# Expert loop of a decoder layer: ids and tables of a block loaded by SyncE, table loads behind the down products, first splits in the last row

## The chip, the cores and the metric

The kernel runs on one core of a Trainium2 chip. The metric is the time of one execution on the device in microseconds, the median of three runs. The engines are TensorE (PE; PEld is its weight load), VectorE (DVE), ScalarE (ACT), GpSimd (POOL) and SyncE (SP), each with its own queue of instructions worked off in order, and 16 DMA engines that carry out the transfers which SP, ACT and POOL issue. Engines wait for one another by semaphores; a DMA adds 16 to its semaphore when it has landed.

## The reference

The input is `x` of 4 rows of 512 tokens with 512 features. The layer adds multi-query attention (16 heads), a selective state-space scan, and a mixture of experts. Only the last part is touched by the change:

```python
logits = x @ gate_weight.T                       # 2048 tokens, 32 experts
topv, topi = jax.lax.top_k(softmax(logits), 8)   # some of the 8 are dropped (weight under 0.05)
...
def expert_step(acc, xs):                        # for each of the 32 experts
    w_gu, w_d, c_e = xs
    g, u = jnp.split(x @ w_gu.T, 2, axis=-1)     # 512 -> 2 x 192
    h = jax.nn.silu(g) * u
    return acc + h @ w_d.T * c_e[:, None], None  # 192 -> 512, times the token's weight
```

## The kernel before

The first part of the program (1373 us) works through the four batch rows: attention, scan and routing of a row, with the next row's beginnings between. At a row's end the tokens are routed: GpSimd scatters an entry for each of a token's choices (`send`, line 1583: 33 floats, namely the token's 32 weights and its number as a float) into `lists`, a table in DRAM with a stretch for each expert. The scatters of the last row come in eight groups `sent0` to `sent7` of four (`send_last`); group k holds each token's k-th choice, counted from the lowest expert, so the list of expert e is complete after groups 0 to e.

The expert loop then works through the lists in blocks of 128 tokens. An expert has at least two blocks; there are 68 here, in 17 quads of four. Which expert and which rows of `lists` a block has is known only at run time: VectorE computes the tables `tab` and `blocks` (in SBUF, line 1508), and every engine reads its loop counts and indices from them by a table load (`value_load`, a load of one number into a register by the engine's queue).

What each engine does for block n:

- SyncE, `load_quad`: loads the 128 entries of each of a quad's four blocks into `meta` (line 429), which has room for all blocks. It may run ahead of the loop, one quad in flight at a time.
- VectorE, `next_ids`: copies the token numbers of block n+4 from `meta` to `get_ids` as whole numbers.
- GpSimd, line 1617 (`get`): gathers the tokens' rows from `xf_dram` into slot n % 4 of `x_blk`, four blocks ahead; line 1623 (`add`): adds the finished rows of `y_ring` to `out` in DRAM by a DMA that accumulates. An add waits until the add two blocks before has landed; the first add of an expert waits until all earlier ones have landed, since a token can be in several experts' lists.
- TensorE, `quad`: at the head of a quad five table loads (line 783), then for each block: `gate_up` of block n+1 (12 matmuls in three parts of split precision, lines 760 to 762), `xt`, the transposes of block n+2 (line 451), `down` of block n (five matmuls, lines 775 to 779), `ht`, the transposes of the hidden values of block n+1.
- ScalarE: `silu`, `xt` (high part of the transposed block), `weigh` (line 1091 copies the ids for the add, line 1093 writes the weighted result to `y_ring`), `ht`. For every expert it also splits the weights, `w_hi` from `w_raw` (line 1073), and issues the weight loads (`load_part`, line 973: 384 and 896 KB), each behind a wait for the load before.
- VectorE: low parts `xt_lo`, `ht_lo`, `w_lo` (`split`, line 1514), and `hidden`, the product of the two halves.

The weights of expert e are loaded four experts ahead, split three (ScalarE) and two (VectorE) ahead. Those of the first experts are loaded in the last row, but split after it, when the routing is done.

Of the kernel before, what the change touches and what calls it, by code (L numbers as in the profile page):

```python
# [26 lines left out]
P = 128  # L27
# [20 lines left out]
T_MORE, T_BEFORE, T_LAST = 0, NE, 2 * NE  # L48
# [28 lines left out]
EXP_BLK = NTOK // P + QUAD - 1  # L77
MAX_BLK = (NTOK * TOPK // P + MIN_BLK * NE + QUAD - 1) // QUAD * QUAD
# [26 lines left out]
def constants():  # L105
# [12 lines left out]
    c[:, C_ALL + NE::LIST_COLS] = NTOK + (p[:, None] * PADS + np.arange(PADS)[None, :]) % P  # L118
# [3 lines left out]
def decoder_layer(nc, a):  # L122
    ctx = ExitStack()
    with ctx:
# [9 lines left out]
        bank = [ctx.enter_context(nc.psum_tensor(f"bank{i}", [P, 512], F32)) for i in range(8)]  # L134
# [31 lines left out]
        xn_hi, xn_lo = sb("xn_hi", [P, KT, T], F32R), sb("xn_lo", [P, KT, T], F32R)  # L166

# [11 lines left out]


        k_t = sb("k_t", [P, T])
        k_hi, k_lo = sb("k_hi", [P, T], F32R), sb("k_lo", [P, T], F32R)
        v_aug = sb("v_aug", [P, TT, DH + 1])
        q_s = sb("q_s", [P, TT, 4, DH])
        q_t = sb("q_t", [P, 2, T])
        q_hi, q_lo = sb("q_hi", [P, 2, T], F32R), sb("q_lo", [P, 2, T], F32R)
        probs = sb("probs", [P, KT, T])
        o_s = sb("o_s", [P, TT, DH])
        k_n = o_s
        o_t = sb("o_t", [P, H, T])  # L190
        wout = sb("wout", [P, 4, D])
        delta = sb("delta", [P, ET, T])
        du = sb("du", [P, ET, T])
        y = sb("y", [P, ET, T])
        decay = sb("decay", [P, ET * (T + DC - 1)])
        x_pad = decay[:, :].rearrange("p (e t) -> p e t", e=ET)
        dA = decay[:, 0:ET * T]
        dA3 = dA.rearrange("p (e t) -> p e t", e=ET)
        dbu = sb("dbu", [P, ET, T])
        state = sb("state", [P, ET, T])  # L200
        b_bc = sb("b_bc", [P, 2, T])
        c_bc = sb("c_bc", [P, 2, T])
        x_dbl = sb("x_dbl", [XD, T])
        junk = sb("junk", [P, 4, DH], mybir.dt.bfloat16)
# [32 lines left out]
        def sb(name, shape, dt=F32):  # L237
# [8 lines left out]
        meta = sb("meta", [P, MAX_BLK + EXP_BLK + QUAD + 1, LIST_COLS])  # L246
        get_ids, add_ids = sb("get_ids", [P, QUAD], I32), sb("add_ids", [P, QUAD], I32)
        xt_hi, xt_lo = sb("xt_hi", [P, KT, P], F32R), sb("xt_lo", [P, KT, P], F32R)
# [21 lines left out]
            w_in meta_in blk_in0 blk_in1 blk_in2 blk_in3  # L270
# [3 lines left out]
            carry_ok ids_ok added0 added1  # L274
# [25 lines left out]
        def span(eng, e):  # L300

            return (eng.value_load(tab[0:1, bass.ds(e, 1)], min_val=MIN_BLK - 1, max_val=EXP_BLK - 1),
                    eng.value_load(tab[0:1, bass.ds(e + T_BEFORE, 1)], min_val=0, max_val=MAX_BLK))

# [16 lines left out]
        def _(sp):  # L321
# [101 lines left out]
            def load_quad(q):  # L423

                rows = [sp.value_load(blocks[0:1, bass.ds(q * QUAD + (B_ROW + i), 1)], min_val=0, max_val=LIST_ROWS - P) for i in range(QUAD)]
                if not (isinstance(q, int) and q == 0):
                    wait_apart(sp, S["meta_in"], q * (QUAD * 16))
                for i in range(QUAD):
                    sp.dma_start(meta[:, bass.ds(q * QUAD + i, 1), :].rearrange("p o c -> p (o c)"), lists[bass.ds(rows[i], P), :]).then_inc(S["meta_in"], 16)
# [5 lines left out]
            early = TOPK * MIN_BLK // QUAD  # L435
            for q in range(early):
                for k in range(QUAD // MIN_BLK * q, QUAD // MIN_BLK * (q + 1)):
                    sp.wait_ge(S[f"sent{k}"], TT * 16)
                load_quad(q)
            with sp.Fori(early, last_quad + 2) as q:  # L440
                load_quad(q)

            wait_apart(sp, S["meta_in"], last_quad * (QUAD * 16) + 2 * QUAD * 16)
            sp.wait_ge(S["w_in"], NE * 2 * 16)
# [4 lines left out]
        def _(pe):  # L449
# [289 lines left out]
            xt_bank, gu_bank, ht_bank, y_bank = bank_q[0], bank_s[0], bank_s[1], bank_o[0]  # L739
            pe.wait_ge(S["carry_ok"], NB)  # L740
            pe.matmul(bank_q[1][:, 0:NE], ones, carry[:], start=True, stop=True).then_inc(S["cnt_ps"], 1)
# [6 lines left out]
            def xt(q, r):  # L748

                wait_apart(pe, S[f"blk_in{r}"], q * 16 + 16)  # L750
                for k in range(KT):
                    mm = transpose(xt_bank[:, k * P:(k + 1) * P], x_blk[:, r, k * P:(k + 1) * P])
                mm.then_inc(S["xt_ps"], 1)

            def gate_up(blk, e):
                hi, lo = gate_up_w(w_hi, e), gate_up_w(w_lo, e)
                pe.wait_ge(S["wlo_ok"], e * 2 + 2)
                pe.wait_ge(S["xtlo_ok"], blk + 1)
                for k in range(KT):
                    pe.matmul(gu_bank[:, 0:2 * INTER], xt_hi[:, k, :], hi[:, k, :], start=(k == 0), stop=False)  # L760
                    pe.matmul(gu_bank[:, 0:2 * INTER], xt_hi[:, k, :], lo[:, k, :], start=False, stop=False)  # L761
                    mm = pe.matmul(gu_bank[:, 0:2 * INTER], xt_lo[:, k, :], hi[:, k, :], start=False, stop=(k == KT - 1))  # L762
                mm.then_inc(S["gu_ps"], 1)
# [17 lines left out]
            def quad(q, last):  # L781

                es = [pe.value_load(blocks[0:1, bass.ds(q * QUAD + (B_EXPERT + i), 1)], min_val=0, max_val=NE - 1) for i in range(QUAD + 1)]
                for r in range(QUAD):
                    blk = q * QUAD + r
                    ends = last and r == QUAD - 1
                    if not ends:
                        gate_up(blk + 1, es[r + 1])
                        xt(q + (r + 2) // QUAD, (r + 2) % QUAD)
                    down(blk, es[r])  # L790
                    if not ends:
                        ht(blk + 1)

# [3 lines left out]
            first = pe.value_load(blocks[0:1, B_EXPERT:B_EXPERT + 1], min_val=0, max_val=NE - 1)  # L797
            xt(0, 0)
            gate_up(0, first)
            xt(0, 1)  # L800
            ht(0)
# [5 lines left out]
        def _(act):  # L807
# [161 lines left out]
            def load_part(e, part):  # L969

                if not (isinstance(e, int) and e + part == 0):
                    act.wait_ge(S["w_in"], (e * 2 + part) * 16)
                act.dma_start(part_w(w_raw, e, part, N_RAW),
                              a["w_exp"][bass.ds(e, 1), :, W_PARTS[part][0]:W_PARTS[part][1]].rearrange("o p n -> (o p) n")).then_inc(S["w_in"], 16)
# [36 lines left out]
            def row(b, at, last):  # L1011
# [57 lines left out]
            xt_bank, gu_bank, ht_bank, y_bank = bank_q[0], bank_s[0], bank_s[1], bank_o[0]  # L1069

            def split(e, part):
                act.wait_ge(S["w_in"], (e * 2 + part + 1) * 16)
                act.activation(part_w(w_hi, e, part, N_SPLIT), part_w(w_raw, e, part, N_RAW), ACT.Copy).then_inc(S["whi_ok"], 1)

            def xt(blk):
                act.wait_ge(S["xt_ps"], blk + 1)
# [617 lines left out]
```

## Time and profile before

| | |
|---|---|
| median of three runs | 1858.85 us (1858.75 to 1859.49) |
| profiled execution: its time | 1863.07 us |
| its span, first to last instruction | 1861.3 us |
| TensorE busy over the span | 80% |
| VectorE busy | 70% |
| ScalarE busy | 51% |
| GpSimd busy | 26% |
| granted TensorE clock, mean | 0.887 |

The times in the rows are microseconds from the first instruction of the one profiled execution. In the timeline a row has the start, the length, engine, line of the kernel, operation, what is written from what, and in brackets how long the engine was idle before and what it waited for; "issue" is a wait for nothing that the profile shows. An engine's name with a q is its queue. A row of the windows view gives the stretch, its length, the busy time of PE, PEld, DVE, ACT and POOL with the number of instructions, the granted TensorE clock as a share of 2.4 GHz, the DMA engines' busy share and GB/s.

### The profile page before, as it was taken

The page shows a single profiled execution, that of the slowest core. Times are in us where ns is not written, and L with a number is a line of the kernel's source. Part 1 is how long each engine was busy: PE and PEld are TensorE (multiplying, and loading weights), DVE is VectorE, ACT ScalarE, POOL GpSimd, SP SyncE. Part 2 cuts the span into 40 slices and gives each one's busy share as a digit, 9 for nine tenths or more (in the row PEclk, how much of TensorE's full clock was granted, in tenths as well). Part 3 has the DMA queues.
Part 4 walks back from the last instruction along what each step waited for, and adds up shares of the span by engine and source line. Part 5 has one row for each costly group of instructions (what it writes and reads, how often), then busy time and mean ns, then how long its engine had stood idle before and what let it go on. Part 6 is the DMA issues. An engine that isn't in the chain of part 4 may idle for free.

```text
span 1861.3 us, 27828 instructions
## 1 busy us (share of the span) xinstructions
PE 1480.5 (80%) x6758; PEld 1056.7 (57%) x6759; DVE 1306.4 (70%) x1908; ACT 954.9 (51%) x2447; POOL 489.8 (26%) x309
## 2 busy tenths in 40 slices
PE   4888889769888986888899597889535777787776
PEld 1677655357665534676654475664224666666664
DVE  6599987559998846899874687986452455555553
ACT  4677743337775244677624465762122444554543
POOL 0000000008700000880000078000036444444454
PEclk8899999869999985999998598999756988988898
DMA  6783231223333113134221413215102777676764
GB/s 250 263 234 85 85 95 41 80 94 73 92 100 85 46 47 131 40 88 114 87 62 34 149 37 82 79 45 157 62 24 58 180 177 191 166 174 166 170 147 58
DMA packets 96495, 202.28 MB, mean 109 GB/s; under 512 B 24984, under 2 KB 26473, under 8 KB 95264
## 3 DMA queue, kind: packets, MB, share of 16 engines
q1 hardware_dynamic: 54960, 86.66, 16.2%
q0 software_dynamic: 28000, 63.84, 14.4%
q10 hardware_dynamic: 13456, 50.87, 9.3%
q8 instruction: 33, 0.54, 0.1%
q14 instruction: 46, 0.38, 0.1%
HBM read 171.06 MB, written 46.21 MB: 117 GB/s over the span
## 4 chain that ended last, share of the span: by engine, by line
DVE 32%; PE 30%; issue 21%; ACT 8%; POOL 2%; DMA 2%; DVEq 2%; ACTq 1%; SPq 0%; another core or an unknown queue 0%; POOLq 0%
DVE state L1267 10%; PE bank L634 8%; DVE y L1277 6%; DVE dbu L1272 5%; PE bank L451 4%; PE bank L760 3%; POOL lists L1583 2%; PE bank L761 2%; PE bank L762 2%; PE bank L594 2%; DVE dbu L1261 2%; DMA w_raw<-in_w_exp 2%; ACT decay L911 1%; PE bank L662 1%; PE bank L518 1%
## 5 line engine op out<-in xcount | busy, mean ns | idle before, releaser
L1583 POOL DMA_INDIRECT lists<-entry,slot x128 | 262.8, 2054 | 395.1 <-DVE slot L1455 207.0
L1267 DVE TENSOR_TENSOR_SCAN state<-decay,dbu 128x2048 f32<-128x2048 f32 x64 | 282.5, 4415 | 7.3 <-ACT decay L911 2.8
L594 PE MATMUL bank<-v_aug,probs 128*128 128x129 f32 x2048 | 250.2, 281 | 7.2 <-ACT probs L905 7.2
L594 PEld LDWEIGHTS bank<-v_aug,probs 128*128 128x128 f32 x2048 | 243.7, 196 | 18.2 <-ACT probs L905 15.2
L634 PE MATMUL bank<-wout,o_t 128*128 128x512 f32 x512 | 234.3, 612 | 0.0
L905 ACT ACTIVATE probs<-bank 128x512 f32<-128x512 f32 x256 | 146.5, 609 | 167.9 <-PE bank L576 129.6
L1579 POOL DMA_DIRECT2D wq<-wq_dram x30 | 21.7, 727 | 735.8 <-PE bank L528 668.7
L911 ACT ACTIVATE decay<-delta,neg_a 128x511 f32<-128x511 f32 x256 | 163.9, 728 | 27.4 <-DVE state L1267 27.4
L760 PE MATMUL bank<-w_hi,xt_hi 128*128 x272 | 113.3, 417 | 81.2 <-issue 58.5
L1623 POOL DMA_INDIRECT out<-y_ring,add_ids x68 | 120.3, 1769 | 202.9 <-ACT y_ring L1093 127.9
L634 PEld LDWEIGHTS bank<-wout,o_t 128*128 128x128 f32 x512 | 98.8, 197 | 123.4 <-issue 123.1
L1261 DVE TENSOR_TENSOR dbu<-du,b_bc 128x2048 f32<-128x2048 f32 x64 | 146.5, 2289 | 6.2 <-DVE rs_r L1147 2.3
L1277 DVE TENSOR_TENSOR y<-y,dbu 128x2048 f32<-128x2048 f32 x64 | 146.7, 2292 | 3.2
L1272 DVE TENSOR_TENSOR dbu<-state,c_bc 128x2048 f32<-128x2048 f32 x64 | 146.7, 2292 | 2.2
L526 PE MATMUL bank<-wq,xn_hi 128*128 128x512 f32 x256 | 109.9, 429 | 28.3 <-DVE q_lo L1227 12.8
L576 PE MATMUL bank<-q_t,k_t 128*128 128x512 f32 x256 | 125.7, 635 | 7.2 <-ACT q_t L893 7.2
L760 PEld LDWEIGHTS bank<-w_hi,xt_hi 128*128 128x128 f32 x272 | 60.3, 222 | 92.9 <-issue 91.8
L761 PE MATMUL bank<-w_lo,xt_hi 128*128 x272 | 105.4, 387 | 3.1 <-issue 3.1
L762 PE MATMUL bank<-w_hi,xt_lo 128*128 x272 | 104.0, 382 | 0.0
L528 PE MATMUL bank<-wq,xn_lo 128*128 128x512 f32 x256 | 102.5, 400 | 0.0
L527 PE MATMUL bank<-wq,xn_hi 128*128 128x512 f32 x256 | 102.0, 398 | 0.0
L1525 DVE TENSOR_TENSOR h_sb<-silu_g,bank 128x128 f32<-128x128 f32 x68 | 19.5, 287 | 115.5 <-ACT silu_g L1081 109.1
(230 smaller groups left out, 2838.7 us busy)
## 6 DMA issues: line engine op xcount, KB each, us to landing
wq<-wq_dram POOLq DMA_DIRECT2D x30, 1024.0 KB
w_raw<-in_w_exp ACTq DMA_DIRECT2D x32, 896.0 KB
wout<-in_wout SPq DMA_DIRECT2D x64, 256.0 KB, 2.7
b_bc<-bc_dram SPq DMA_DIRECT2D x64, 256.0 KB
c_bc<-bc_dram SPq DMA_DIRECT2D x64, 256.0 KB
w_raw<-in_w_exp ACTq DMA_DIRECT2D x32, 384.0 KB
lists<-in_const ACTq DMA_DIRECT2D x1, 8712.0 KB, 49.1
q_s<-in_x SPq DMA_DIRECT2D x4, 1024.0 KB, 7.7
```

Source lines behind the costliest of these rows:

```text
L594: mm = pe.matmul(bank_o[half][:, (t % 2) * (DH + 1):(t % 2 + 1) * (DH + 1)], probs[:, k, t * P:(t + 1) * P], v_aug[:, k, :], start=(k == 0 ...
L634: mm = pe.matmul((bank_o + bank_s)[t][:], o_t[:, h, t * P:(t + 1) * P], wout[:, h % 4, :], start=(h == 0), stop=(h == H - 1))
L760: pe.matmul(gu_bank[:, 0:2 * INTER], xt_hi[:, k, :], hi[:, k, :], start=(k == 0), stop=False)
L761: pe.matmul(gu_bank[:, 0:2 * INTER], xt_hi[:, k, :], lo[:, k, :], start=False, stop=False)
L762: mm = pe.matmul(gu_bank[:, 0:2 * INTER], xt_lo[:, k, :], hi[:, k, :], start=False, stop=(k == KT - 1))
L905: act.activation(probs[:, k, :], bank_s[k % 2][:], ACT.Exp).then_inc(S["exp_ok"], 1)
L911: act.activation(dA3[:, e, 1:], delta[:, e, 1:], ACT.Exp, scale=neg_a[:, bass.ds(n, 1), e:e + 1].rearrange("p a c -> p (a c)")).then_inc(S ...
L1261: dve.tensor_tensor(dbu[:], du[:], b_bc[:, fill[0]:fill[0] + 1, :].to_broadcast([P, ET, T]), ALU.mult).then_inc(S["dbu_ok"], 1)
L1267: dve.tensor_tensor_scan(state[:].rearrange("p e t -> p (e t)"), dA, dbu[:].rearrange("p e t -> p (e t)"), 0.0, ALU.mult, ALU.add).then_in ...
L1272: dve.tensor_tensor(dbu[:], state[:], c_bc[:, i:i + 1, :].to_broadcast([P, ET, T]), ALU.mult).then_inc(S["bc_free"], 1)
L1277: dve.tensor_tensor(y[:], y[:], dbu[:], ALU.add).then_inc(S["y_ok"], 1)
L1583: pool.indirect_dma_start(out=lists, out_offset=bass.IndirectOffsetOnAxis(ap=slot[:, t, k:k + 1].bitcast(U32), axis=0), in_=entry[:, t, :] ...
```

## The change

- The token number in an entry is stored as a whole number's bits, so that it can be used as an index without a conversion.
- `meta` is a ring of eight blocks of weights only. For each block SyncE loads the 32 weights of each token and, in two more DMAs of 4 bytes for each of 128 partitions, the ids for the gather (`get_ids`) and the ids for the add (`add_ids`). The copies by VectorE (`next_ids`) and ScalarE (line 1091) go.
- GpSimd gathers six blocks ahead of the add in place of four, as soon as the block in the slot has been transposed. The scatters of groups 3 to 7 stand among the first gathers and adds.
- TensorE transposes three blocks ahead in place of two, into two PSUM banks by turns (`pair`); `xt_hi` and `xt_lo` are doubled. It reads one expert number for each block, behind the down product; the wait for the landed add four blocks back moves from ScalarE to ahead of the down product.
- ScalarE and VectorE read one number for each expert in place of two, and at the end of the expert before.
- Weight loads have a semaphore for each part, and the waits between them go. The splits of the first experts move into the last row; SBUF tensors are laid out in another order for that.

The core of the diff:

```diff
+        pair = ctx.enter_context(nc.psum_tensor("pair", [P, 2, 512], F32))
-        meta = sb("meta", [P, MAX_BLK + EXP_BLK + QUAD + 1, LIST_COLS])
+        meta = sb("meta", [P, N_META, NE])          # N_META = 2 * QUAD
-        xt_hi, xt_lo = sb("xt_hi", [P, KT, P], F32R), sb("xt_lo", [P, KT, P], F32R)
+        xt_hi, xt_lo = sb("xt_hi", [P, 2, KT, P], F32R), sb("xt_lo", [P, 2, KT, P], F32R)
...
 SyncE
+            def load_get(q, r, row):
+                sp.dma_start(meta[:, bass.ds((q * QUAD + r) % N_META, 1), :].rearrange("p o c -> p (o c)"), lists[bass.ds(row, P), 0:NE]).then_inc(S[f"get_in{r}"], 16)
+                sp.dma_start(get_ids[:, r:r + 1], lists[bass.ds(row, P), NE:].bitcast(I32), allow_slow_non_contiguous=True).then_inc(S[f"get_in{r}"], 16)
+            def load_add(r, row):
+                sp.dma_start(add_ids[:, r:r + 1], lists[bass.ds(row, P), NE:].bitcast(I32), allow_slow_non_contiguous=True).then_inc(S[f"add_in{r}"], 16)
+            def load_quad(q, early=False):
+                for r in range(QUAD):
+                    if early and r % MIN_BLK == 0:
+                        sp.wait_ge(S[f"sent{(q * QUAD + r) // MIN_BLK}"], TT * 16)
+                    row = list_row(q, r)
+                    first = early and q == 0
+                    if not first:
+                        wait_apart(sp, S[f"blk_in{r}"], q * 16)
+                    load_get(q, r, row)
+                    if first:
+                        load_add(r, row)
+                    elif not (early and q == 1 and r < QUAD - 1):
+                        behind = (r + 1) % QUAD
+                        aq = q if r == QUAD - 1 else q - 1
+                        row = list_row(aq, behind)
+                        wait_apart(sp, S[f"added{behind % 2}"], aq * 32 + (ADDED0 + (behind // 2 - 1) * 16))
+                        load_add(behind, row)
...
 TensorE
-                es = [pe.value_load(blocks[0:1, bass.ds(q * QUAD + (B_EXPERT + i), 1)], ...) for i in range(QUAD + 1)]
+                es = [pe.snap(e_now, ...), pe.snap(e_next, ...)]
                 for r in range(QUAD):
                     if not ends:
-                        gate_up(blk + 1, es[r + 1])
-                        xt(q + (r + 2) // QUAD, (r + 2) % QUAD)
+                        gate_up(blk + 1, es[r + 1], (r + 1) % 2)
+                        xt(q + (r + 3) // QUAD, (r + 3) % QUAD)
+                    wait_apart(pe, S[f"added{r % 2}"], q * 32 + (ADDED0 + (r // 2 - 1) * 16))
                     down(blk, es[r])
                     if not ends:
+                        es.append(expert_of(q, r + 2))
                         ht(blk + 1)
...
 ScalarE
             def load_part(e, part):
-                if not (isinstance(e, int) and e + part == 0):
-                    act.wait_ge(S["w_in"], (e * 2 + part) * 16)
...
                 if last:
                     for e in range(4):
                         for part in range(2):
+                            if e > 0:
+                                act.wait_ge(S[f"w_in{part}"], e * 16)
                             load_part(e, part)
+                    for e in range(3):
+                        for part in range(2):
+                            split(e, part)
...
 VectorE, last row, behind the last state_sum
+                if last:
+                    dve.wait_ge(S["oT_ok"], NB * H)
+                    for e in range(2):
+                        for part in range(2):
+                            split(e, part)
...
 GpSimd
+            def get_next(q, r):
+                far = r + QUAD + 2
+                fq, fr = far // QUAD, far % QUAD
+                wait_apart(pool, S[f"get_in{fr}"], q * 32 + (fq * 32 + 32))
+                wait_apart(pool, S["xt_ps"], q * QUAD + (far - QUAD + 1))
+                get(fr)
+            def add_next(q, r):
+                landed = pool.value_load(blocks[0:1, bass.ds(q * QUAD + (B_LANDED + r), 1)], ...)
+                wait_apart(pool, S[f"add_in{r}"], q * 16 + 16)
+                wait_apart(pool, S[f"added{r % 2}"], q * 32 + (ADDED0 + (r // 2) * 16))
+                wait_apart(pool, S[f"added{(r + 1) % 2}"], landed)
+                wait_apart(pool, S["yb_ok"], q * QUAD + (r + 1))
+                add(r)
...
+            for q in range(2):
+                for r in range(QUAD):
+                    if r % 2 == 0 and q * 2 + r // 2 + 3 in range(4, TOPK):
+                        k = q * 2 + r // 2 + 3
+                        send_last(range(k, k + 1))
+                    get_next(q, r)
+                    add_next(q, r)
+            send_last(range(TOPK - 1, TOPK))
+            with pool.Fori(2, last_quad) as q:
+                for r in range(QUAD):
+                    get_next(q, r)
+                    add_next(q, r)
```

## Rows read from the trace of the kernel before

**Rows 1.** Windows view, one stretch of the expert loop (columns explained above)

```profile
1586.00:1689.00 103.00, 80.87 (x373) 66.04 (x372) 54.30 (x114) 52.53 (x97) 47.51 (x32) 0.87 0.70 172
```

**Rows 2.** Timeline of TensorE, one quad: start, us, line, operation, idle before

```profile
1625.39 0.44 PE L451 MATMUL bank<-const,h_sb 128*128 128x128 f32 x2 [0.39 <-DVE h_sb L1527]
...
1630.24 0.68 PE L760 MATMUL bank<-w_hi,xt_hi 128*128 x1 [4.41 <-issue]
...
1634.09 0.60 PE L451 MATMUL bank<-const,x_blk 128*128 128x128 f32 x4
...
1641.55 0.44 PE L760 MATMUL bank<-w_hi,xt_hi 128*128 x1 [0.30 <-DVE xt_lo L1519]
...
1643.77 0.60 PE L451 MATMUL bank<-const,x_blk 128*128 128x128 f32 x4
...
1655.34 0.68 PE L760 MATMUL bank<-w_hi,xt_hi 128*128 x1 [4.41 <-issue]
```

**Rows 3.** Line 783: table loads on TensorE's queue between two quads

```profile
L783 PEldq TENSOR_LOAD <-blocks x5: 296/307/482, 1599.7 to 1603.0; - x5
```

**Rows 4.** Timeline: adds and gathers of GpSimd, one weighted block of ScalarE

```profile
1440.02 1.59 POOL L1623 DMA_INDIRECT out<-y_ring,add_ids  x1 [2.90 <-ACT y_ring L1093]
...
1463.65 1.59 POOL L1623 DMA_INDIRECT out<-y_ring,add_ids  x1 [0.94 <-ACT y_ring L1093]
...
1465.99 1.06 POOL L1617 DMA_INDIRECT x_blk<-xf_dram,get_ids  x1 [0.76 <-issue]
...
1470.91 2.02 POOL L1623 DMA_INDIRECT out<-y_ring,add_ids  x1 [3.86 <-DMA out<-y_ring,add_ids]
...
1484.30 1.59 POOL L1623 DMA_INDIRECT out<-y_ring,add_ids  x1 [6.76 <-ACT y_ring L1093]
...
1615.47 0.69 ACT L1093 ACTIVATE y_ring<-bank,meta 128x512 f32 x1 [0.74 <-PE bank L779]
...
1617.07 1.59 POOL L1623 DMA_INDIRECT out<-y_ring,add_ids  x1 [1.01 <-ACT y_ring L1093]
...
1825.29 1.59 POOL L1623 DMA_INDIRECT out<-y_ring,add_ids  x1 [0.30 <-issue]
...
1831.38 1.59 POOL L1623 DMA_INDIRECT out<-y_ring,add_ids  x1 [3.15 <-DMA out<-y_ring,add_ids]
...
1852.09 1.59 POOL L1623 DMA_INDIRECT out<-y_ring,add_ids  x1 [0.86 <-ACT y_ring L1093]
```

**Rows 5.** Timeline of VectorE and ScalarE: end of last row, first splits

```profile
1319.27 1.49 DVE L1156 BATCH_NORM_STATS2 st<-bank 128x6 f32<-128x512 f32 x2 [28.78 <-PE bank L634]
...
1322.79 0.21 ACT L810 ACTIVATE rs_l<-mv 128x4 f32<-128x4 f32 x1 [45.86 <-DVE mv L1159]
...
1372.63 7.07 ACT L1073 ACTIVATE w_hi<-w_raw 128x768 fp32r<-128x768 f32 x6 [11.96 <-DVE slot L1455]
...
1383.60 5.68 DVE L1514 TENSOR_TENSOR w_lo<-w_raw,w_hi 128x768 fp32r<-128x768 f32 x4
```

**Rows 6.** Chain that ended last: the wait for a weight load's landing

```profile
1591.68 3.44 DMA w_raw<-in_w_exp
```

**Rows 7.** SyncE: table loads (line 425), first four DMAs, the copy they released

```profile
L425 SPq TENSOR_LOAD <-blocks x4: 146/261/268, 1384.8 to 1386.4; - x4
...
1387.12 1.99 SPq L429 DMA_DIRECT2D meta<-lists  x4
...
1390.55 0.17 DVE L1546 CAST get_ids<-meta 128x4 int32<-128x4 f32 x1 [1.28 <-DMA meta<-lists]
```

**Rows 8.** Timeline at the loop's start, and the scatter's DMA issue row

```profile
1383.27 0.40 DVE L1509 CAST blocks<-bank 1x256 int32<-1x256 f32 x1
...
1396.85 0.98 POOL L1583 DMA_INDIRECT lists<-entry,slot  x1 [0.30 <-issue]
...
1399.42 1.04 POOL L1617 DMA_INDIRECT x_blk<-xf_dram,get_ids  x1 [0.30 <-issue]
...
lists<-entry,slot POOLq DMA_INDIRECT x128, 2.1
```

More of the change, by code:

```diff
@@ L420, in _, with list_row @@
             each_row(sp, row)
[L423 to L429, printed above, removed]
+            def list_row(q, r):
+                return sp.value_load(blocks[0:1, bass.ds(q * QUAD + (B_ROW + r), 1)], min_val=0, max_val=LIST_ROWS - P)
+            def load_get(q, r, row):
[3 more added lines that the diff above has]
+                sp.dma_start(add_ids[:, r:r + 1], lists[bass.ds(row, P), NE:].bitcast(I32), allow_slow_non_contiguous=True).then_inc(S[f"add_in{r}"], 16)
             sp.wait_ge(S["rows_ok"], 2)
@@ L433, in _ @@
             sp.wait_ge(S["sent"], (NB - 1) * SENT)
[L435 to L438, printed above, removed]
-                load_quad(q)
[L440 to L444, printed above, removed]
+            def load_quad(q, early=False):
[15 more added lines that the diff above has]
+                        load_add(behind, row)
+            for q in range(TOPK * MIN_BLK // QUAD):
+                load_quad(q, True)
+            with sp.Fori(TOPK * MIN_BLK // QUAD, last_quad + 2) as q:
+                load_quad(q)
+            for r in range(QUAD):
+                wait_apart(sp, S[f"get_in{r}"], last_quad * 32 + 64)
+                wait_apart(sp, S[f"add_in{r}"], last_quad * 16 + (32 if r == 0 else 16))
+            for part in range(2):
+                sp.wait_ge(S[f"w_in{part}"], NE * 16)
             sp.wait_ge(S["x2_out"], NB * 16)
@@ L781, in quad @@
             def quad(q, last):
-                es = [pe.value_load(blocks[0:1, bass.ds(q * QUAD + (B_EXPERT + i), 1)], min_val=0, max_val=NE - 1) for i in range(QUAD + 1)]
+                es = [pe.snap(e_now, min_val=0, max_val=NE - 1), pe.snap(e_next, min_val=0, max_val=NE - 1)]
                 for r in range(QUAD):
@@ L1357, in row @@
                     state_sum(b, n)
+                if last:
+                    dve.wait_ge(S["oT_ok"], NB * H)
+                    for e in range(2):
+                        for part in range(2):
+                            split(e, part)
                 if not last:
@@ new lines, in _ @@
+            for r in range(2):
+                pool.wait_ge(S[f"get_in{r}"], 32)
+                get(r)
+            send_last(range(2, 3))
+            for r in range(2, QUAD):
+                pool.wait_ge(S[f"get_in{r}"], 32)
+                get(r)
+            send_last(range(3, 4))
+            for r in range(2):
+                get_next(-1, r + 2)
+            last_quad = pool.value_load(tab[0:1, T_LAST:T_LAST + 1], min_val=NE * MIN_BLK // QUAD - 1, max_val=MAX_BLK // QUAD - 1)
+            pool.wait_ge(S["x2_out"], NB * 16)
@@ new lines, in _ @@
+            for q in range(2):
[7 more added lines that the diff above has]
+            with pool.Fori(2, last_quad) as q:
+                for r in range(QUAD):
+                    get_next(q, r)
+                    add_next(q, r)
```

194 lines of the change are left out of this document (94 added, 100 removed).

## The prediction

> **What bounds the kernel now.** I read the page first for the clock and DMA shares, then the stretches of the expert loop, then one quad on TensorE, then GpSimd and SyncE. The loop, from the first gather to the last row, is 460 of the 1861 us and holds nearly everything the change touches. In it TensorE is busy 79% and the DMA engines 70% [rows 1]. What ends last is TensorE: each quad of four blocks begins with a hole of 4.41 us that no semaphore explains [rows 2]. In such a hole five table loads run on TensorE's queue, starting from 1599.7 to 1603.0, 0.82 us apart [rows 3]. The clock pays too: the gate-up product behind a hole takes 1630.24 to 1634.09, 3.85 us, at 1.2 GHz for most of it; a warm one 1641.55 to 1643.77, 2.22 us. A quad is 1630.24 to 1655.34, 25.1 us: four warm blocks of 4.8, the hole, 1.6 for the clock.
>
> Second, hidden now: the adds of finished blocks. The first add of an expert waits until all earlier adds have landed. One such add starts 7.26 us after the start of the add it waited for; a gather is issued between [rows 4]. Late in the loop, with the weight loads over, it was 6.09. GpSimd wakes 0.91 us after its releaser: the weighted block ends at 1616.16, the add starts at 1617.07. So an add lands 6.35 us after its start, 5.18 in the quiet case.
>
> I number the 68 blocks and adds from 0: add 1 starts at 1440.02, add 8 at 1484.30, add 63 at 1831.38, add 67 at 1852.09, and the span ends 9.2 later. Adds 8 to 63 are 27.5 pairs of 12.62 us.
>
> **Edit by edit.** *Splits in the last row.* Before, ScalarE's six first splits take 7.07 us at 1372.6 and VectorE's four 5.68 us at 1383.6 [rows 5]. In the last row VectorE is idle 28.78 us and ScalarE 45.86 us before their next row [rows 5]; both wait for TensorE's output product, so the splits cost nothing there. Without that cover they would cost up to 12.8.
>
> *Weight loads without waits, transposes three ahead, two banks.* The wait behind each weight load ended with the landing 3.44 us after the issue [rows 6], just as ScalarE came by: worth about nothing. The transposes ahead take away the 0.30 that a gate-up product waits for the low part [rows 2]; ScalarE and VectorE lose a small copy of ids each. All this is on engines that do not end last after the change, so I count 0; were TensorE the bound, it would be 0.3 a block.
>
> *Table loads behind the down products.* One load a block, 0.82 us, issued when five down matmuls are already in the queue. Bounds: 0 if the queue runs ahead, 0.82 a block if not; TensorE then needs 5.6 a block at most. The hole and its cold clock go: 6.0 us in each of 16 quads, 96 us if nothing else binds.
>
> *The tables of a block by SyncE.* This is the part I take to bind. Before, four 16.5 KB loads a quad ran far ahead; after, each block has three small loads (weights of the block, ids for the gather, ids for the add), in order on SyncE. Follow one round. In SyncE's step m the loads for gather m come first; then it waits until add m-7 has landed and loads the ids of add m-3. GpSimd issues gather n+6 ahead of add n. The loads for gather n+6 stand behind step n+5's wait, which is for add n-2. So **add n cannot start until add n-2 has landed, SyncE has issued three loads, the last of them has landed, and gather n+6 has been issued.** Two blocks cost one such round T:
>
> - landing of add n-2 from its start: 6.35 [rows 4]
> - SyncE: four table loads start from 1384.8 to 1386.4, 0.53 apart, with the step to the DMA about 0.6; four DMAs take 1.99, so 0.5 each [rows 7]. One table load and three DMAs: 2.1
> - landing of the last small load: the nearest row is a quiet 1.44, from the issue's end (1389.11) to the copy it released (1390.55) [rows 7]; the other bound is 3.44, a weight load's landing [rows 6]. The engines are 70% busy, so I take 3.0, near the loaded one
> - GpSimd wakes: 0.91
> - gather 1.06 and 0.30 to the next instruction: 1.36 [rows 4]
>
> T = 6.35+2.1+3.0+0.91+1.36 = 13.7 us, 6.85 a block, against 12.62 a pair now. Ends: 5.18+2.1+1.44+0.91+1.36 = 11.0, and with the loop's landing and 3.44 it is 14.2.
>
> The Trainium skill ("DMA: Bandwidth & Descriptors", section "Anatomy of one DMA") puts a fixed cost of about 2.0 us on a DMA of any size. The quiet row agrees (1.9 from the last issue's start to the copy); with the page's figure in place of the 3.0 T would be about 12.2, an estimate. Its section "Issuing engines are not separate DMA queues" says that loads of all issuers interleave on the same 16 engines, which speaks for the longer landing; no row here shows a single small load under load.
>
> **The start.** Now the first gather is issued at 1399.42, behind 16 scatters, each 0.98 with 0.30 before it, so 1.28 [rows 8]. After, it needs eight, and its own ids: the tables' row numbers are there at 1383.67, SyncE's first DMA came 3.45 later at 1387.12 with five table loads before it; with three fewer 1385.5; two DMAs 1.0, landing 1.44, wake 0.91: 1388.9. So everything up to add 1 comes 10.5 earlier: add 1 at 1429.5. But the remaining scatters now stand among the first adds, four before every second add, and the next gather's ids can be read only when these have landed. A pair there is: add, gap, gather, gap 3.25; add and gap 1.9; scatters 5.1; their landing (2.1 from the start [rows 8]) 0.8 more; SyncE 0.6+1.0+3.0; wake 0.9; gather 1.36: 17.9. Add 2 is at 1429.5+1.9+5.1+0.8+4.6+0.9+1.36 = 1444.2, add 8 three pairs on, at 1498: 13.7 later than now.
>
> **Sum.** 1498 + 27.5 x 13.72 = 1875; add 63 to 67 as now 20.7, end 9.2: span 1905, 43.4 more than 1861.3. The profiled execution's own time is 1863.07, 4.2 above the median of 1858.85; the difference goes onto the median: **1902 us**.
>
> **Rivals.**
> *The plan works* (0.11): the small loads are never last. Then the expert-boundary wait binds: 7.26+1.59+0.30+1.06+0.30 = 10.5 a pair, and TensorE (9.6 warm) fits below. Start 10.5 earlier, add 8 at 1473.8: 1473.8+289+29.9 = 1793, so 1790 us. For it: the hole is real and large. Against: the order of waits above.
> *The round is short* (0.11): T at its low end 11.0, landing 1.44 at the start too (add 8 at 1491.8): 1824, so 1822 us. Against: that landing is from a stretch with little DMA. The round decides here: from T about 12.2 down the kernel gets faster.
> *A draw* (0.08): loop landings of adds, quiet small ones, T = 12.16: 1857, so 1855 us.
> *The clock* (0.04): TensorE now waits about 2 us in every block, at the down product. If that kept it at 1.2 GHz, a warm block of 4.8 becomes 4.8 x 3.85/2.22 = 8.3: 1498+55 x 8.3+30 = 1985, about 1980 us. Against: such a TensorE would not wait, and the warm rows of [rows 2] show 2.4 GHz granted within 4 us of unbroken work.
> *Forecast* (0.66): own range 1868 to 1932; T = 14.2 gives 1917, and the start may be worse.
>
> Under 0.2% (about what a measurement of this kernel can tell from no change) is "same": 1855 to 1862.6. The draw and the edge of its neighbours give 0.08; faster takes the first two rivals, 0.22; slower 0.70. The range runs from just under the short round to the forecast's upper end, 1815 to 1938, and leaves out the working plan, the clock and a little of the tail.
>
> **What would show it.** Right: in TensorE's rows no hole at the quad's start, a wait at the first down matmul in most blocks (no longer a gate-up one), add 8 near 1498, pairs of adds 13.7 apart, GpSimd's gathers ended idle by small loads of ids, DMA share in the loop lower than 0.70, first gather near 1389. The splits lie before 1319. Wrong: pairs near 10.5 and GpSimd waiting only on adds; then the landing of small loads was mis-sized or the chain through SyncE is not closed as I read it.

## The result, and the profile after

| | before | after |
|---|---|---|
| median | 1858.80 us (1854.98 to 1859.49, 4 runs) | 1902.74 us (1896.32 to 1907.43, 4 runs) |
| profiled execution: time, span | 1863.07, 1861.3 us | 1896.32, 1894.5 us |
| granted TensorE clock, mean | 0.887 | 0.881 |

The ratio is 1.0238 (95% interval 1.0203 to 1.0274): the change makes the kernel 44 us slower. The profiled execution of after is the shortest of its four, and that of before is 4 us above its median, so the two traces differ by 33 us and not by 44.

The page names the cause. The part that lists the chain that ended last, by engine and by line, gives 15% of it to DMA (the page of before has 2%), and behind the adds come the small loads of ids and SyncE's queue:

```profile
DVE 29%; issue 21%; PE 18%; DMA 15%; ACT 8%; SPq 4%; POOL 3%; POOLq 1%; DVEq 1%; ACTq 0%
DVE state L1310 10%; DMA out<-y_ring,add_ids 9%; PE bank L661 8%; DVE y L1320 5%; DMA get_ids<-lists 5%; DVE dbu L1315 5%; POOL lists L1628 2%; PE bank L621 2%; ACT decay L951 2%; PE bank L478 2%; DVE dbu L1304 1%; PE bank L603 1%; SPq L428 1%; PE pair L545 1%; PE bank L689 1%
```

One round of that chain, 1601.56 to 1615.08 (start, length, what; short pieces left out):

```profile
1601.56 5.22 DMA out<-y_ring,add_ids
...
1607.00 0.33 SPq L436
...
1607.85 0.73 SPq L428
...
1609.23 0.35 SPq L432
...
1609.78 2.74 DMA get_ids<-lists
...
1613.79 0.18 POOL x_blk L1662
...
1615.08 5.44 DMA out<-y_ring,add_ids
...
1622.61 3.78 DMA get_ids<-lists
```

It reads as the prediction has it: an add lands, SyncE issues the ids for an add (L436), reads the table (L428), loads weights (L432) and ids (L433) of the next block, the ids land, GpSimd issues the gather (L1662) and then the add that stood behind it. Two blocks a round.

TensorE has no hole at the quad's start any more. It waits for gathered rows instead, ahead of the transposes. First its timeline, then its groups from 1500 to 1850 (busy and mean ns, then idle time before them and what ended it):

```profile
1670.36 0.34 PE L789 MATMUL bank<-w_hi,xt_lo 128*128 x1
1674.65 0.63 PE L478 MATMUL pair<-const,x_blk 128*128 128x128 f32 x4 [3.96 <-DMA x_blk<-xf_dram,get_ids]
...
1688.58 0.68 PE L478 MATMUL pair<-const,x_blk 128*128 128x128 f32 x4 [3.67 <-DMA x_blk<-xf_dram,get_ids]
```

```profile
L787 PE MATMUL bank<-w_hi,xt_hi 128*128 x201 | 76.5, 380 | 0.0
...
L478 PE MATMUL pair<-const,x_blk 128*128 128x128 f32 x200 | 37.0, 316 | 88.4 <-DMA x_blk<-xf_dram,get_ids 88.4
```

The same stretch as [rows 1], with fewer matmuls in it and the DMA engines just as busy:

```profile
1586.00:1689.00 103.00, 73.56 (x331) 57.66 (x329) 48.24 (x88) 43.27 (x72) 46.51 (x31) 0.87 0.71 165
```

Against [rows 4], adds 1, 2, 8, 63 and 67 of after, from GpSimd's timeline:

```profile
1417.14 1.59 POOL L1668 DMA_INDIRECT out<-y_ring,add_ids  x1 [0.31 <-issue]
...
1431.38 1.61 POOL L1668 DMA_INDIRECT out<-y_ring,add_ids  x1 [0.30 <-issue]
...
1490.78 1.61 POOL L1668 DMA_INDIRECT out<-y_ring,add_ids  x1 [1.11 <-issue]
...
1871.68 1.59 POOL L1668 DMA_INDIRECT out<-y_ring,add_ids  x1 [2.63 <-issue]
...
1886.85 1.55 POOL L1668 DMA_INDIRECT out<-y_ring,add_ids  x1 [2.53 <-issue]
```

Adds 8 to 63 are 27.5 pairs of 13.85 us; before, 12.62. That is 33.8 us, the whole of what the traces show. Add 8 comes 6.5 later than before, and the end from add 63 on is 7 shorter.

### The profile page after: what moved, and what is told of

Same layout as the page of the kernel before. It is cut to its first block, busy times and chain, and to the rows that moved or that the text cites. A ratio compares the mean times of both kernels' runs of the same rounds, so it can differ in the third digit from the quotient of the medians.

```text
span 1894.5 us, 28141 instructions
## 1 busy us (share of the span) xinstructions
PE 1487.9 (79%) x6762; PEld 1056.3 (56%) x6763; DVE 1299.6 (69%) x1839; ACT 939.9 (50%) x2380; POOL 486.3 (26%) x307
## 4 chain that ended last, share of the span: by engine, by line
DVE 29%; issue 21%; PE 18%; DMA 15%; ACT 8%; SPq 4%; POOL 3%; POOLq 1%; DVEq 1%; ACTq 0%
DVE state L1310 10%; DMA out<-y_ring,add_ids 9%; PE bank L661 8%; DVE y L1320 5%; DMA get_ids<-lists 5%; DVE dbu L1315 5%; POOL lists L1628 2%; PE bank L621 2%; ACT decay L951 2%; PE bank L478 2%; DVE dbu L1304 1%; PE bank L603 1%; SPq L428 1%; PE pair L545 1%; PE bank L689 1%
## 5 line engine op out<-in xcount | busy, mean ns | idle before, releaser
L1568 DVE TENSOR_TENSOR xt_lo<-pair,xt_hi (+1 forms) x70 | 48.4, 691 | 168.4 <-ACT xt_hi L1120 168.2
L478 PE MATMUL pair<-const,x_blk 128*128 128x128 f32 x280 | 52.7, 321 | 135.8 <-DMA x_blk<-xf_dram,get_ids 135.8
L1662 POOL DMA_INDIRECT x_blk<-xf_dram,get_ids x70 | 80.5, 1149 | 221.7 <-issue 173.3
L1120 ACT ACTIVATE xt_hi<-pair (+1 forms) x70 | 41.9, 599 | 185.9 <-PE pair L478 185.8
L553 PE MATMUL pair<-wq,xn_hi 128*128 128x512 f32 x256 | 110.2, 430 | 28.0 <-DVE q_lo L1270 12.7
L478 PEld LDWEIGHTS pair<-const,x_blk 128*128 128x128 f32 x280 | 38.5, 163 | 147.0 <-issue 135.6
L787 PE MATMUL bank<-w_hi,xt_hi 128*128 x272 | 104.1, 383 | 2.7 <-DVE xt_lo L1568 2.7
L555 PE MATMUL pair<-wq,xn_lo 128*128 128x512 f32 x256 | 102.8, 402 | 0.0
```

Of the source, the lines that this page charges most:

```text
L478: return pe.transpose(out, src, ident)
```

## The experiments

T is the start of add 63 less that of add 8, by 27.5, from each profiled execution. Ratios are to the kernel before on the same chip.

| kernel | median us | ratio (95%) | T | add 8 |
|---|---|---|---|---|
| before | 1858.8 | 1 | 12.62 | 1484.30 |
| after | 1902.7 | 1.0238 (1.0203 to 1.0274) | 13.85 | 1490.78 |
| e4: after, two more small loads | 1936.4 | 1.0385 (1.0365 to 1.0405) | 14.79 | 1503.93 |
| e8: after, table loads at the head | 1916.9 | 1.0261 (1.0216 to 1.0306) | 14.34 | 1502.15 |
| e2: after, add ahead of gather | 1843.9 | 0.9878 (0.9857 to 0.9898) | 12.30 | 1488.68 |
| e1: after, ids for the add later | 1822.4 | 0.9772 (0.9748 to 0.9796) | 10.92 | 1499.09 |
| e3: e1 and e2 | 1800.8 | 0.9676 (0.9611 to 0.9741) | 10.09 | 1486.54 |
| e7: e3, splits behind the row | 1792.6 | 0.9625 (0.9572 to 0.9678) | 10.29 | 1485.03 |
| e6: e3, scatters first | 1791.0 | 0.9597 (0.9553 to 0.9640) | 10.24 | 1485.11 |
| e9: e3, e6 and e7 | 1783.3 | 0.9596 (0.9558 to 0.9634) | 10.71 | 1475.11 |
| e5: before, table loads behind | 1798.0 | 0.9634 (0.9595 to 0.9673) | 10.53 | 1483.41 |
| e12: e5 again | 1785.4 | 0.9605 (0.9591 to 0.9619) | 10.49 | 1468.50 |
| e10: e5, no waits of weight loads | 1796.0 | 0.9656 (0.9617 to 0.9695) | 11.13 | 1469.04 |
| e11: e5, gathers early | 1785.8 | 0.9611 (0.9599 to 0.9624) | 10.49 | 1468.57 |

The first scatter of the last row starts anywhere from 1372.26 to 1383.41 in these traces, behind parts of the program that most of the experiments don't touch; a start is to be compared only by what lies behind that scatter, and a few us of one execution are no finding. Three kernels vary by 22 to 24 us from execution to execution: e3 (1789.7 to 1813.9, the trace is of a short one), e9 (1775.2 to 1799.2, of a long one) and e10 (1785.7 to 1808.1, of a long one). Their T is that of one such execution.

**e1, the ids for an add a step later** (`meta` has room for 16 blocks, since weights are loaded further ahead of their use):

```diff
-                    elif not (early and q == 1 and r < QUAD - 1):
-                        behind = (r + 1) % QUAD
-                        aq = q if r == QUAD - 1 else q - 1
-                        row = list_row(aq, behind)
-                        wait_apart(sp, S[f"added{behind % 2}"], aq * 32 + (ADDED0 + (behind // 2 - 1) * 16))
-                        load_add(behind, row)
+                    elif not (early and q == 1):
+                        row = list_row(q - 1, r)
+                        wait_apart(sp, S[f"added{r % 2}"], (q - 1) * 32 + (ADDED0 + (r // 2 - 1) * 16))
+                        load_add(r, row)
```

> Made from the changed kernel: SyncE loads the ids for an add one step later, in step m those of add m-4 (behind the landing of add m-8) in place of those of add m-3 (behind add m-7). The number and size of all transfers stay the same. Theory S (the round through SyncE sets the pace): add n then hangs on add n-3 in place of n-2, so that the 13.85 us round is shared by three blocks, 4.6 each; what binds then is the wait at an expert's first add or TensorE, 10.5 to 11.5 us a pair. 27.5 pairs give back 65 to 92 us: 1811 to 1838 us, and the wait of TensorE's transposes for gathered rows goes. Rival D (it is the number of small transfers that slows everything): no change, 1895 to 1905. Rival G (a gather waits for its slot in x_blk, the adds are not in it): no change.

1822.4 us: 80 less than after (87 by the ratios), with the same transfers. T falls to 10.92. This is the test of the round; the number of small loads can't be what costs nearly all of the loss, since e1 has the same number.

**e2, the add ahead of the gather:**

```diff
             with pool.Fori(2, last_quad) as q:
                 for r in range(QUAD):
-                    get_next(q, r)
                     add_next(q, r)
+                    get_next(q, r)
```

> Made from the changed kernel: in GpSimd's loop add n is issued ahead of gather n+6 and no longer behind it. SyncE is as in the changed kernel. Theory S: add n then needs only the tables of gather n+5, which hang on add n-3: the same opening of the round as with the ids a step later, 1811 to 1840 us. Rival D (number of small transfers): 1895 to 1905. Rival G (gathers are late by themselves): the gathers come one add later still, TensorE's wait for gathered rows grows, over 1905 us.

1843.9, a little above the range, T 12.30. The round opens here too, but less than in e1: TensorE still waits 49.7 us for gathered rows from 1500 to 1770, in e1 35.2. That each gather now comes behind an add fits this; it was not tried by itself. Rival G, which gave over 1905, is out.

**e3, both.**

> Made from the changed kernel: both edits, the ids for an add loaded a step later and the add issued ahead of the gather. Theory S: add n hangs on add n-4; the round (13.85 us over four blocks) is far below every other bound, so the time is that of either edit alone within 1 per cent, and the new bound, the first adds of experts at 10.5 a pair or TensorE, is seen undisturbed: 1805 to 1835. If it is still well below the single edits, the round bound those too. Rival D: 1895 to 1905.

1800.8, T 10.09: well below both single edits, outside the 1% that was expected, so by the reading given beforehand the round still bound those, and four blocks to a round free it. The stretch of [rows 1] in e3:

```profile
1586.00:1689.00 103.00, 95.30 (x488) 75.21 (x489) 67.09 (x126) 62.07 (x106) 58.69 (x44) 1.00 0.95 232
```

488 matmuls in place of 373 before and 331 after, full clock, DMA share 0.95. GpSimd's timeline shows what is left, every second add waiting for the landing of one before, 9.8 us a pair:

```profile
1608.80 1.59 POOL L1666 DMA_INDIRECT out<-y_ring,add_ids  x1 [0.30 <-PE pair L476]
1610.70 1.06 POOL L1660 DMA_INDIRECT x_blk<-xf_dram,get_ids  x1 [0.31 <-issue]
1614.99 1.59 POOL L1666 DMA_INDIRECT out<-y_ring,add_ids  x1 [3.24 <-DMA out<-y_ring,add_ids]
1616.88 1.40 POOL L1660 DMA_INDIRECT x_blk<-xf_dram,get_ids  x1 [0.31 <-issue]
1618.59 1.59 POOL L1666 DMA_INDIRECT out<-y_ring,add_ids  x1 [0.30 <-issue]
```

**e4, two more small loads in SyncE's step:**

```diff
+                for i in range(2):     # q > 0
+                    sp.dma_start(spare[:, r * 2 + i:r * 2 + i + 1], lists[bass.ds(row, P), NE:].bitcast(I32), ...).then_inc(S[f"spare_in{r}"], 16)
                 sp.dma_start(meta[...], lists[bass.ds(row, P), 0:NE]).then_inc(S[f"get_in{r}"], 16)
```

> Made from the changed kernel: ahead of the two loads for gather m SyncE issues two more loads of 4 bytes for each of 128 partitions, into a tile that nobody reads. Theory S: each adds its issue of 0.5 us to the round of two blocks: 27.5 x 1.0 = 27 us and a few more at the start, 1925 to 1940. Theories by which SyncE has slack: no change. Rival D: the small transfers go from three to five a block; if they are what cost the 75 to 110 us that the hole did not give, that makes 50 to 75 us more, 1955 to 1980.

1936.4. By the ratios it is (1.0385 - 1.0238) x 1858.85 = 27 us above after, and T grew by 0.94, about the two issues of 0.5. SyncE's issuing time is in the round, and beyond their issue the extra transfers cost nothing that these runs can tell. Its queue's own rows (the x2 is the pair of extra loads):

```profile
1600.27 0.33 SPq L440 DMA_DIRECT2D add_ids<-lists  x1
1602.44 0.81 SPq L435 DMA_DIRECT2D spare<-lists  x2
1603.51 0.35 SPq L436 DMA_DIRECT2D meta<-lists  x1
1603.95 0.38 SPq L437 DMA_DIRECT2D get_ids<-lists  x1
```

**e5 and e12, the kernel before with the table loads behind the down products alone:**

```diff
-                es = [pe.value_load(blocks[0:1, bass.ds(q * QUAD + (B_EXPERT + i), 1)], ...) for i in range(QUAD + 1)]
+                es = [pe.snap(e_now, ...), pe.snap(e_next, ...)]
...
                     down(blk, es[r])
                     if not ends:
+                        es.append(expert_of(q, r + 2))
                         ht(blk + 1)
```

> Made from the kernel before: only TensorE's table loads move, one for each block behind its down product, none at the head of a quad. Nothing else of the change is in it. If the hole binds as read, 4.41 us and 1.6 of clock in each of 16 quads go, until the next bound: the first adds of experts (10.5 a pair) or TensorE with 0.8 of table load in each block (11.2 a pair). 27.5 pairs of 12.62 less 10.5 to 11.2 give back 39 to 58 us: 1802 to 1822 us. If the hole was a cover for the adds' wait (they bind before too), little goes: 1845 to 1860.

> The kernel before with TensorE's table loads behind the down products and nothing else, once more (1798.0 in its first run, ratio 0.9634) beside the next three, with more rounds. By every theory 1795 to 1801, and pairs of adds 10.5 apart: the wait at an expert's first add.

1798.0, and 1785.4 in the second run: 68 and 73 us less than before by the ratios, more than the 39 to 58 expected, and the second run lies 10 us below the 1795 to 1801 expected for it. T is 10.53 and 10.49, the 10.5 that the prediction's first rival works out for the first adds of experts; in e12 27.5 x 2.1 = 58 us is the loop's share, 5 more come from the end (add 63 to 67 takes 15.5 in place of 20.7), the rest from the start. What sets the 10.5 is open: every second add waits for the landing of an earlier one (below), but the chain that ended last of e12, from 1500 to 1760, gives 39% to the landings of weight loads on which ScalarE waits before it issues the next. The table loads lie in no gap of TensorE: from 1500 to 1770 its gate-up products of e12 waited for the low part 12.0 us in all and for "issue" 0.3 at most. Stretch of [rows 1] in e12, and a pair of adds:

```profile
1586.00:1689.00 103.00, 92.17 (x453) 72.06 (x453) 65.11 (x138) 62.16 (x118) 53.38 (x40) 0.98 0.87 215
```

```profile
1599.16 1.59 POOL L1633 DMA_INDIRECT out<-y_ring,add_ids  x1 [0.30 <-issue]
1601.05 1.06 POOL L1627 DMA_INDIRECT x_blk<-xf_dram,get_ids  x1 [0.30 <-issue]
1606.12 1.59 POOL L1633 DMA_INDIRECT out<-y_ring,add_ids  x1 [4.01 <-DMA out<-y_ring,add_ids]
...
1609.37 1.59 POOL L1633 DMA_INDIRECT out<-y_ring,add_ids  x1 [0.30 <-issue]
```

**e8, after with the table loads at the head again** (the five loads as before, the two registers out).

> Made from the changed kernel: only TensorE's table loads go back, five at the head of a quad. Theory S: a quad of the changed kernel is two rounds of 13.85, 27.7 us, and TensorE with the hole needs 25.1; it has 2.6 us to spare in each quad, so the time stays, within 10 us of 1900. If the hole was gone for good and its 4.4 us were a gain that the round ate only in part, it comes back: 16 x 4.4 = 70 us, 1970.

1916.9, on a chip where before takes 1864.1: 1.0261 against 1.0238, intervals overlapping, 4 us by the ratios. In after, the hole's removal is worth too little to be told, since TensorE waits for rows anyway: in e8, from 1500 to 1780, the gate-up products wait 18.7 us for "issue" and the transposes 57.6 us for gathered rows. T is 0.5 longer than in after; e8's trace is of its longest execution and that of after of its shortest, so no more is read from it. The same edit is worth 70 us on the kernel before (e12). The other parts of the change together took that gain and 44 us more.

**e6, scatters ahead of the first add, on e3:**

```diff
             for r in range(2):
                 get_next(-1, r + 2)
+            send_last(range(4, TOPK))
...
-                    if r % 2 == 0 and q * 2 + r // 2 + 3 in range(4, TOPK):
-                        k = q * 2 + r // 2 + 3
-                        send_last(range(k, k + 1))
                     get_next(q, r)
                     add_next(q, r)
-            send_last(range(TOPK - 1, TOPK))
```

> Made from the fastest so far, the changed kernel with both edits (ids for an add a step later, add ahead of the gather; 1800.8): the scatters of groups 4 to 7 stand ahead of the first add, right behind the sixth gather, and none between the adds. In the kernel with both edits adds 1 to 7 come at a pair in 15 to 19 us (1421.19 to 1479.43). Theory that scatters among the adds make the start slow: 16 scatters of 1.28 delay add 0 by up to 20 us, to 1436, but its pairs then take 10 to 11, so that add 8 comes at 1436 + 4 x 10.5 = 1478 in place of 1486.5: 8 us faster, 1785 to 1798. Rival (the landing of the lists and the small loads make the start slow, not the scatters' place): pairs stay at 15 and more, and the time grows by 10 to 20 us.

The mechanism shows: add 0 at 1436.67, the next pairs at 1448.28, 1459.20, 1471.79 and 1485.11, so 10.9 to 13.3 apart, where e3 has 19.0, 22.3, 19.1 and 10.4. From its first scatter to add 8 it is 106.4 us, in e3 110.9. The times, 1791.0 and 1800.8, have overlapping intervals: 10 us by the medians, 15 by the ratios, 4.5 by that stretch of the traces. That the pairs close up is seen; how much of the time it saves is not settled.

**e7, first splits behind the last row,** on both engines, on e3.

> Made from the changed kernel with both edits (1800.8): the first splits stand behind the last row again, on ScalarE and VectorE, as before the change. If they cost nothing in the last row and lay beside the scatters before, as the prediction has it for both places, the time stays within 5 us. If their place was worth something (before, the first gate-up of block 1 took 10.95 us, 1415.75 to 1426.7, and a scatter beside VectorE's splits 6.34 in place of 0.98), 5 to 17 us are lost: 1806 to 1818, with the slow scatter and the slow first gate-up back in the trace. If the splits in the last row cost what they take, 7.07 on ScalarE, the time falls by up to 7.

1792.6 against 1800.8 with overlapping intervals: the loss of 5 to 17 us is not seen, and whether it is no change or the gain of up to 7 can't be told. The slow first gate-up of block 1 is not back (from 1402.20, without a gap). One instruction is slowed, as in before. VectorE's four splits and the first gather of e7:

```profile
1383.81 5.67 DVE L1363 TENSOR_TENSOR w_lo<-w_raw,w_hi 128x768 fp32r<-128x768 f32 x4
...
1388.63 1.78 POOL L1658 DMA_INDIRECT x_blk<-xf_dram,get_ids  x1 [4.93 <-DMA get_ids<-lists]
```

For nearly all of the splits GpSimd is waiting for ids in any case, so beside the gathers they cost little.

**e10, the kernel of e5 with a semaphore for each part of the weights and no wait between the loads of the loop:**

```diff
             def load_part(e, part):
-                if not (isinstance(e, int) and e + part == 0):
-                    act.wait_ge(S["w_in"], (e * 2 + part) * 16)
-                act.dma_start(...).then_inc(S["w_in"], 16)
+                act.dma_start(...).then_inc(S[f"w_in{part}"], 16)
```

> The kernel before with the table loads behind the down products, and the weight loads with a semaphore for each part and no wait between them. The prediction's step has this at nothing: the same as the kernel with the table loads alone, within 3 us. Rival (the wait on ScalarE holds up silu, hidden values and y_ring behind it, 32 experts and two waits each): with TensorE's hole gone it shows, 10 to 30 us less.

Neither, as far as can be told: 1796.0 against e12's 1785.4 and 0.9656 against 0.9605, the intervals just overlapping, and e5, the same kernel as e12, had 0.9634. The gain of 10 to 30 us is out; a loss of some 10 us is possible, not shown. The trace is of an execution of 1801.8. The transfers' rows, 1500 to 1770, first e12, then e10 (KB each, then median us from issue to landing where the trace gives one), and TensorE's transposes of e10:

```profile
out<-y_ring,add_ids POOLq DMA_INDIRECT x53, 6.0
x_blk<-xf_dram,get_ids POOLq DMA_INDIRECT x52, 4.8
```

```profile
w_raw<-in_w_exp ACTq DMA_DIRECT2D x21, 896.0 KB, 7.4
...
out<-y_ring,add_ids POOLq DMA_INDIRECT x49, 5.3
x_blk<-xf_dram,get_ids POOLq DMA_INDIRECT x48, 7.0
```

```profile
L452 PE MATMUL bank<-const,x_blk 128*128 128x128 f32 x192 | 30.6, 284 | 32.4 <-DMA x_blk<-xf_dram,get_ids 32.3
```

A gather lands after 7.0 us in place of 4.8, and TensorE waits 32.3 us for rows where e12 waits 0.1. The weight loads overlap in this trace: a large one lands after 7.4 us, and the next load is mostly issued 3 to 6.5 us behind it. That this is what makes the gathers late is not shown: e9 has no waits between the loads either, and its gathers land after 4.8 us.

**e11, first gathers ahead of the later scatters,** on e5: gathers 0 and 1 behind three groups of scatters, 2 and 3 behind the fourth.

> The kernel before with the table loads behind the down products, and the first gathers ahead: gathers 0 and 1 behind three groups of scatters in place of four, gathers 2 and 3 behind the fourth, the other four groups behind them, all before the first add. In the kernel with the table loads alone the first gather comes at 1406.4, add 0 at 1438.9. If the gathers set the start: first gather 6 us earlier, the fourth 14 us earlier, add 0 bound by the scatters (the last ends at about 1429) and about 1432; 5 to 8 us less than the table loads alone, about 1790 to 1793. If the start is bound by the wait at each expert's first add (two blocks an expert, 10.5 a pair) from add 0 on: the same 5 to 8. If it is bound by the scatters' end alone: within 2 us.

1785.8 against 1785.4 for e12: no gain that can be told. The first gather comes at 1394.05 (e12 1398.27), add 0 at 1427.48 (e12 1425.73). That fits the last of the three cases expected, the start bound by the scatters' end.

**e9, the edits of e3, e6 and e7 on after.**

> The changed kernel with all the edits tried on it: ids for an add a step later, add ahead of the gather, scatters ahead of the first add, splits behind the last row. If round and start are all that the change loses by, it is now bound by the same wait at experts' first adds as the kernel with the table loads alone, and some of its blocks by TensorE (9.6 a pair): 1780 to 1795, equal to or up to 15 us better than the table loads alone. If the small transfers cost something of their own, it stays 5 to 10 us behind it.

1783.3, ratio 0.9596 against 0.9605 for e12. No version beats the one that moves the table loads alone by more than the runs can tell.

## Why the prediction was right, by its steps

**The round.** T was forecast at 13.72 and is 13.85. Its terms, in the round from 1601.56 and the next one: landing of the add until SyncE goes on 5.3 and 5.5 (forecast 6.35; over the loop an add lands after 5.6 by the median); SyncE to its last issue 2.9 and 2.0 (2.1); landing of the ids 2.74 and 3.78 (3.0; over the whole loop 2.9, below); GpSimd to the gather 1.1 and 1.05 (0.91); gather to add 1.4 and 1.75 (1.36). The add's landing was put about 1 us too long and the other terms together as much too short, so the closeness of the sum is in part luck; the order of the waits is not. e1, e3 and e4 show the mechanism: shared by more blocks it goes away, lengthened by 1.0 it costs 0.94.

The term with the widest bounds was the small load's landing. The transfers' rows of after, 1500 to 1860:

```profile
meta<-lists SPq DMA_DIRECT2D x52, 16.0 KB, 2.8
get_ids<-lists SPq DMA_DIRECT2D x52, 0.5 KB, 2.9
...
add_ids<-lists SPq DMA_DIRECT2D x51, 0.5 KB, 2.7
```

The loaded landing was the right choice, twice the quiet 1.44 of [rows 7]. The Trainium skill ("DMA: Bandwidth & Descriptors", section "Anatomy of one DMA") has about 2.0 us for any size, but for transfers that GpSimd issues, which the prediction leaves out; these are SyncE's, and under this loop's load the trace has 2.7 to 2.9.

**The start.** The first gather was forecast at 1388.9 and came at 1389.82. Add 8 was forecast at 1498 and came at 1490.78, by two misses of opposite sign. Add 1 came at 1417.14 in place of 1429.5: the step that only shifts the start by the gather's 10.5 missed that before, the first quad's first gate-up takes 1415.75 to 1426.7, with a gap of 0.4 to 0.8 us after one matmul and after two by turns. The last of these in before, and e8's two:

```profile
1425.70 0.66 PE L761 MATMUL bank<-w_lo,xt_hi 128*128 x1 [0.73 <-issue]
```

```profile
1414.77 0.66 PE L788 MATMUL bank<-w_lo,xt_hi 128*128 x1 [0.17 <-issue]
1416.15 0.66 PE L787 MATMUL bank<-w_hi,xt_hi 128*128 x1 [0.40 <-issue]
```

Of all the kernels only before and e8 have such gaps, the two with table loads at the quad's head; whether and how the loads slow the matmuls behind them stays open. Add 2 came 14.2 behind add 1 (forecast 14.7), but the three pairs from add 2 took 59.4 us where 3 x 17.9 = 53.7 were forecast.

**The end.** Add 63 to 67 took 15.17 in place of the 20.7 carried over from before. In all the other kernels it is 14.8 to 16.4. e12 differs from before in the table loads alone and has 15.5, so the loads' place is behind the 20.7 there; but e8 has them at the head too, beside the round, and 15.0, so what makes the difference stays open. I took the 20.7 over unexamined.

So the span is 1894.5 against 1905: add 8 came 7 us early, the loop took 4 more, the end 7 less. The median of 1902.74 against 1902 is luck beyond that. The forecast took the median to lie 4 us below the profiled time, as in before; in after it lies 6 above, since the shortest execution was profiled. (1905 less 1861.3 is 43.7 and not 43.4, which changes nothing.)

**Splits in the last row.** At 1293.87 (7.08 us) and 1294.85 (two groups, 0.96 and 4.83), VectorE then idle 19.31 until 1320.47, 1.2 later than in [rows 5]: no cost seen there, and in e7 none that can be told.

**Waits of the weight loads** were priced at nothing. e10, where TensorE is nearly bound, doesn't refute it and doesn't confirm it: a loss of some 10 us is possible there. In after gathers land after 4.2, and no cost of this step can be seen beside the round.

**What would show it.** Right: no hole at the quad's start, pairs 13.85 apart where 13.7 were forecast, GpSimd's gathers behind the ids in the chain. Wrong: TensorE waits at the transposes, not at the first down product. I had put the landed add four blocks back as what is late for TensorE, but gather n+6 is issued behind the same round as add n and lands later than the add that the down product asks for. And the DMA share is 0.71, where one below 0.70 was forecast, at 165 GB/s in place of 172: from 1500 to 1860 SyncE's queue has 4.2% of the engines' time, in before 0.6%.

**The rivals.** "The plan works" had 10.5 a pair, which is what e5, e12 and e11 run at (10.49 to 10.53); whether by the wait that this rival names or by the weight loads is open (e12). In the change the round comes first. The short round and the draw fall with the landing of 2.9, the clock with a grant of 0.87 in the loop.

## What to carry to other kernels

When a load that ran far ahead is replaced by one that is issued just in time, write the order of waits of its queue down as a round: who must have landed before the issuer goes on, what it issues then, who stands behind that. The round's length divided by the blocks in flight is a bound like any engine's. Here one more step of distance (e1) gave 80 us, and two more transfers for each block (e4) cost 27.

A change of several parts is to be tried part by part: here one part alone, five table loads moved, gives 70 us, and the other parts took back more.

## What the runs showed of the hardware

**A split on VectorE holds up GpSimd's DMA issue.** In before, the ninth scatter took 6.34 us in place of 0.98 while VectorE ran its four splits (1383.60, 5.68 us):

```profile
1383.79 6.34 POOL L1583 DMA_INDIRECT lists<-entry,slot  x1 [0.30 <-issue]
```

In e5 it took 6.32; in e7 the first gather, begun 0.85 before the splits' end, took 1.78 in place of 1.05. Over all the traces 15 scatters take more than 1.5 us; each lies beside a split, and each ends 0.85 to 0.88 us after that split. The Trainium skill ("GPSIMD Engine Reference", section "1. Specifications") says that GpSimd's interface to SBUF is shared with VectorE and contended by instructions with two SBUF inputs; a split has two, and the trace agrees. The prediction overlooked this in the trace of before, where it delays the first gather by 5.4 us.

**Small loads under load.** With the DMA engines 70% busy, 512 bytes and 16 KB land in the same 2.7 to 2.9 us; between these two sizes there is no difference.

**TensorE's clock follows the gaps.** The grant in the stretch from 1586 to 1689 is 0.87 in before and in after, where TensorE stands idle for 22 and 29 us of 103, and 1.00 in e3 and 0.98 in e12, where it stands idle for 8 and 11.
